# An attention and mixture-of-experts block on one core: query sets by single batches, keys by pairs of batches, the gate's power on GpSimd from tile 2 on, and the last tile's matmuls with the logits' half first

## The reference

```python
x = x + layernorm(attention(layernorm(x)))   # 32 query heads, 8 key heads, head size 16, rotary, causal
x = x + layernorm(ffn(layernorm(x)))
# ffn: x @ W_base.T + b; logits = x @ W_gate.T (8 experts), softmax, top 2, renormalised;
# h = x @ A (8 experts x rank 16), times the route weight of its expert, @ B, added
```

## Time and profile before

| | us |
|---|---|
| median of 3 runs (lowest, highest) | 234.39 (233.6, 234.4) |
| the profiled execution, its own time | 235.09 |
| its span, first to last instruction | 233.4 |
| PE busy | 201.3 (86%) |
| DVE busy | 173.3 (74%) |
| ACT busy | 125.6 (54%) |
| POOL busy | 113.2 (49%) |

### The profile page before, as it was taken

One profiled execution on the slowest core, in us unless ns is written; L12 is line 12 of the kernel. 1 busy time (PEld: TensorE's weight loads), 2 busy tenths in 40 slices (PEclk: granted clock), 3 DMA queues, 4 the chain that ended last, 5 costly groups with the idle time before them and its releaser, 6 DMA issues.

```text
span 233.4 us, 3763 instructions
## 1 busy us (share of the span) xinstructions
PE 201.3 (86%) x1292; PEld 123.5 (53%) x1304; DVE 173.3 (74%) x364; ACT 125.6 (54%) x222; POOL 113.2 (49%) x96
## 2 busy tenths in 40 slices
PE   0499999999787879999999989899889989998860
PEld 0394843444454544444444524144778868997830
DVE  1773525767998897868696884686798898888785
ACT  3231440341214877888766785773577488773321
POOL 8200231562439695798743446462746262433352
PEclk9999999999999999999999999999999999999985
DMA  5998048976996302696673203344330001110113
GB/s 162 383 367 328 0 138 164 233 200 168 202 220 144 66 1 76 165 181 125 143 143 65 48 11 51 101 90 95 51 93 0 3 0 45 46 48 0 45 45 135
DMA packets 22465, 26.73 MB, mean 115 GB/s; under 512 B 3760, under 2 KB 17328, under 8 KB 21680
## 3 DMA queue, kind: packets, MB, share of 16 engines
q1 hardware_dynamic: 22304, 26.38, 44.8%
q10 hardware_dynamic: 144, 0.13, 0.2%
HBM read 17.19 MB, written 6.95 MB: 103 GB/s over the span
## 4 chain that ended last, share of the span: by engine, by line
PE 48%; DVE 22%; ACT 10%; issue 9%; DMA 5%; POOL 3%; SPq 2%; DVEq 0%; POOLq 0%
PE ps L1146 7%; PE ps L1194 7%; PE ps L1131 6%; PE ps L1105 4%; PE ps L1046 4%; PE ps L1169 4%; DVE stats L772 4%; PE ps L1036 3%; DVE nmax L967 3%; PE ps L1022 3%; DVE nmax L964 2%; ACT L577 2%; ACT region_a L719 2%; DMA x_sb<-x 2%; PE ps L1085 2%
## 5 line engine op out<-in xcount | busy, mean ns | idle before, releaser
L543 POOL TENSOR_SCALAR_AFFINE_SELECT region_a<-region_a 128x1024 f32<-128x1024 f32 x32 | 36.9, 1154 | 26.9 <-ACT region_a L719 26.7
L967 DVE TENSOR_REDUCE nmax<-ps 128x4 f32<-128x1024 f32 x32 | 39.1, 1223 | 10.3 <-PE ps L1105 10.0
L719 ACT ACTIVATE region_a<-ps 128x1024 f32<-128x1024 f32 x32 | 32.7, 1022 | 0.2 <-PE ps L1131 0.2
L1036 PE MATMUL ps<-region_a,region_c 128*128 128x512 f32 x64 | 29.0, 598 | 0.0
L1131 PE MATMUL ps<-region_b,kst 98*128 98x512 bf16 x96 | 26.8, 381 | 1.6 <-ACT region_a L719 1.1
L716 ACT ACTIVATE region_a<-ps 128x512 f32<-128x512 f32 x32 | 19.2, 599 | 16.4 <-PE ps L1131 15.9
L964 DVE TENSOR_REDUCE nmax<-ps 128x4 f32<-128x512 f32 x32 | 21.8, 682 | 4.8 <-PE ps L1089 4.4
L1146 PE MATMUL ps<-region_a,v_aug 128*32 128x512 f32 x192 | 25.3, 603 | 0.0
L583 ACT ACTIVATE std<-mv,eps_sb 128x1 f32<-128x1 f32 x32 | 9.3, 293 | 22.4 <-DVE mv L773 22.3
L1105 PE MATMUL ps<-kst,region_b 96*128 96x128 bf16 x256 | 19.6, 219 | 1.4 <-DVE nmax L967 0.8
L462 POOL TENSOR_TENSOR region_a<-region_a 128x512 f32<-128x512 f32 x4 | 6.5, 1627 | 28.9 <-DVE region_a L820 28.9
(11 more groups left out here) (107 smaller groups left out, 415.3 us busy)
## 6 DMA issues: line engine op xcount, KB each, us to landing
q_scr<-region_c SPq DMA_DIRECT2D x24, 128.0 KB, 2.6
region_b<-q_scr SPq DMA_DIRECT2D x8, 384.0 KB, 5.2
x_sb<-x SPq DMA_DIRECT2D x8, 256.0 KB, 5.7
region_b<-q_scr SPq DMA_DIRECT2D x8, 256.0 KB, 5.6
attn_t<-o_sb SPq DMA_DIRECT2D x32, 64.0 KB, 2.4
rden_bc<-r_scr SPq DMA_DIRECT2D x8, 256.0 KB, 3.4
out<-region_b SPq DMA_DIRECT2D x7, 256.0 KB, 2.0
kst<-k_scr SPq DMA_DIRECT2D x8, 192.0 KB, 3.5
```

The costliest lines, as they stand in the source:

```text
L543: pool.affine_select(out=blocks, in_=blocks, compare_op=ALU.is_ge, fill=0.0, base=0, pattern=[[0, 2], [0, REP], [1, P]], channel_multiplie ...
L719: nc.scalar.activation(probs[:, u % PRING, 1:3, :], ps[:, 4:6, :], ACT.Exp, scale=float(HEAD_DIM) ** -0.5).then_inc(exp_done, 1)
L967: nc.vector.tensor_reduce(nmax[:, gi % 2, 1, heads], ps[:, 1:3, :].rearrange("p a (r k) -> p r a k", r=REP), AX.XY, ALU.max, negate=True). ...
L1036: last = nc.tensor.matmul(ps[:, SET_BANKS[i][ri], :], wq_sb[:, c, col:col + P], xn_t[:, c, half * HALF:(half + 1) * HALF], start=(c == 0), ...
```

## The change

Sets are now (kind, index): `("q", b)` is one batch with both groups, `("k", p)` a pair of batches with 256 columns. Order: q0, k0, q1, k1 in front, q2 and q3 in steps 0 to 7 of the loop, a quarter in each. The front's rotation is on VectorE alone; both late sets go over GpSimd. Keys are written without repetition and repeated when loaded, in a ring of three batches. `POWER_TILE` goes from 5 to 2. In the last tile's step TensorE does the second half of the columns first, and `gating_choice` of the last tile moves one step ahead, with its `gate_power`. `attn_low_part` of the last batch moves from step 4 to 5 on GpSimd. The probability slots start at 3 (`slot_of`), and some small tiles share memory.

```diff
+KRING = 3
-LOADS = {7: 4, 15: 5, 18: 6, 22: 7}
+LOADS_Q = {9: 4, 15: 5, 18: 6, 22: 7}
+LOADS_K = {8: 2, 18: 3}
-POWER_TILE = 5
-ROPE_3 = {0: 1, 1: 2}
-MATMULS_4 = (1, 1, 1, 1, 1)
-ROTATE_4, SPLIT_HIGH_4, SPLIT_MIDDLE_4, WRITE_4 = 5, 10, 12, 14
+POWER_TILE = 2
+LATE_PROJECT = 4
+K_ROPE = {0: 0, 1: 1, 2: 2, 3: 3}
+K_HIGH, K_MIDDLE = 2, 3
+LATE_COPY = {2: (2, 0), 4: (2, 1), 6: (3, 0), 8: (3, 1)}
+LATE_ROTATE = {2: 0, 8: 1}
+LATE_HIGH = {6: 4, 10: 5}
+LATE_MIDDLE = {7: 4, 12: 5}
+LATE_WRITE = {7: 2, 14: 3}
...
-        SETS = [(0, 0), "K", (0, 1), (1, 0), (1, 1)]
-        SET_BANKS = [(2, 3), (4, 5), (6, 7), (2, 3), (4, 5)]
+        SETS = [("q", 0), ("k", 0), ("q", 1), ("k", 1), ("q", 2), ("q", 3)]
+        SET_BANKS = [(2, 3), (4, 5), (2, 3), (4, 5), (6, 7), (6, 7)]
...
             sp.dma_start(ident_sb[:, :], ident).then_inc(ident_loaded, 16)
+            sp.dma_start(x_sb[:, 1, :], x[P:2 * P, :]).then_inc(x_loaded[1], 16)
+            sp.dma_start(wq_sb[:, :, :], wq.rearrange("(c p) n -> p c n", p=P)).then_inc(wq_loaded, 16)
+            for t in range(2, TILES):
+                sp.dma_start(x_sb[:, t, :], x[t * P:(t + 1) * P, :]).then_inc(x_loaded[t], 16)
+                if t == 3:
+                    sp.dma_start(tab_sb[:, :, :], tables).then_inc(tab_loaded, 16)
+                    sp.dma_start(wk_sb[:, :, :], wk.rearrange("(c p) n -> p c n", p=P)).then_inc(wk_loaded, 16)
             sp.dma_start(wv_sb[:, :, :], wv.rearrange("(c p) n -> p c n", p=P)).then_inc(wv_loaded, 16)
...
+            def load_k(b):
+                sp.wait_ge(k_written[b], WRITES)
+                if b >= KRING:
+                    sp.wait_ge(t_psum, 2 * KV_HEADS * (b - KRING + 1))
+                for part, (first, count) in enumerate(RUNS):
+                    rows = k_scr[b, part].rearrange("i f h n -> (i f) (h n)")
+                    sp.dma_start(kst[first * HEAD_DIM:(first + count) * HEAD_DIM, b % KRING, :, :],
+                                 rows.unsqueeze(0).broadcast_to([count, HEAD_DIM, KV_HEADS * SEQ]))\
+                        .then_inc(k_loaded[b % KRING], 16)
...
             write_q(0)
+            write_k(0, (0, 1))
             load_q(0)
+            write_k(0, (2,))
+            load_k(0)
+            load_q(1)
+            write_k(1, range(PARTS))
+            write_q(1)
+            load_k(1)
             load_q(2)
             load_q(3)
+            write_k(2, range(PARTS))
+            write_k(3, range(PARTS))
...
 # GpSimd, tile phase
-                if POWER_TILE <= s - 3 < TILES:
+                if POWER_TILE <= s - 3 < TILES - 1:
                     gate_power(s - 3)
+                if s == TILES + 1:
+                    gate_power(TILES - 1)
+                if s == 5:
+                    attn_low_part(BATCH - 1)
...
 # VectorE, front
+            input_tiles(0, 6)
+            dve.wait_ge(tab_loaded, 16)
+            for i in range(2):
+                rope_multiply(i, 0)
+                rope_multiply(i, 1)
+                for piece in (rope_add, rope_left, rope_low):
+                    piece(i, 0)
+                    piece(i, 1)
+            input_tiles(6, TILES)
...
 # VectorE, tile step
                     ln_stats(3, t4, y_sb[:, t4 % 2, :])
+                    if t4 == TILES - 3:
+                        gating_choice(TILES - 1)
...
 # TensorE, front
+            turn_x(0)
+            turn_x(1)
+            project_q(0)
+            turn_x(2)
+            turn_x(3)
+            project_k(0)
+            for t in range(4):
+                project_v(t)
+            project_q(1)
+            for t in range(4, TILES):
+                turn_x(t)
+                if t > 4:
+                    project_v(t - 1)
+            project_v(TILES - 1)
+            project_k(1)
...
 # TensorE, loop
-                if n < len(MATMULS_4):
-                    project(4, 2 * KC - sum(MATMULS_4[n:]), MATMULS_4[n])
+                if n < 2 * LATE_PROJECT:
+                    project_q(2 + n // LATE_PROJECT, (n % LATE_PROJECT,))
...
 # TensorE, tile step
+                if t2 == TILES - 1:
+                    for term in range(3):
+                        base_down_router(t2, term, (1,))
+                    turn_hw(t3)
+                    base_down_router(t2, 0, (0,))
+                    up_projection(t3)
+                    base_down_router(t2, 1, (0,))
+                    turn_hw(t2)
+                    base_down_router(t2, 2, (0,))
+                    up_projection(t2)
+                    return
```

More of the change, by code:

```diff
@@ L50 @@
 RING = 5
+KRING = 3
 PRING = 8
+FIRST_SLOT = 3
 ST_LAG = 9
@@ L184, in build @@
         mask_loaded = sem("mask_loaded")
-        wq_loaded = [sem(f"wq_loaded{g}") for g in range(2)]
+        wq_loaded = sem("wq_loaded")
         tab_loaded = sem("tab_loaded")
@@ new lines, in rope_low @@
+            def rope_low(i, ri):
+                a, cols = i % 2, slice(0, SEQ if SETS[i][0] == "k" else HALF)
+                dve.wait_ge(left, 2 * i + ri + 1)
+                dve.wait_ge(part_m, 2 * i + ri + 1)
+                nc.vector.tensor_tensor(parts[:, a, ri, 2, cols], resid[:, a, ri, cols], parts[:, a, ri, 1, cols],
+                                        ALU.subtract).then_inc(part_l, 1)
+            input_tiles(0, 6)
[6 more added lines that the diff above has]
+                    piece(i, 1)
@@ L1029, in project, with project_q @@
+            def project_q(b, pieces=range(4)):
+                i = SETS.index(("q", b))
+                pe.wait_ge(wq_loaded, 16)
+                pe.wait_ge(xnt_ready, 2 * b + 2)
+                for piece in pieces:
+                    ri, g = divmod(piece, 2)
                     if i == 2:
+                        pe.wait_ge(rope_mul, 2 * ri + 2)
+                    if i == DIRECT:
                         pe.wait_ge(v_ready, 2)
-                    pe.wait_ge(xnt_ready, 4 * half + 4)
-                    for m in range(first, first + count):
-                        ri, c = divmod(m, KC)
-                        col = (2 * g + ri) * P
-                        last = nc.tensor.matmul(ps[:, SET_BANKS[i][ri], :], wq_sb[:, c, col:col + P],
-                                                xn_t[:, c, half * HALF:(half + 1) * HALF],
-                                                start=(c == 0), stop=(c == KC - 1))
@@ L1039, in project @@
-                if first + count == 2 * KC:
-                    last.then_inc(proj_psum, 1)
+                    if i > DIRECT:
+                        pe.wait_ge(late_copied, ri + 1)
+                    col = (2 * g + ri) * P
+                    for c in range(KC):
+                        last = nc.tensor.matmul(ps[:, SET_BANKS[i][ri], g * SEQ:(g + 1) * SEQ], wq_sb[:, c, col:col + P],
+                                                xn_t[:, c, b * SEQ:(b + 1) * SEQ], start=(c == 0), stop=(c == KC - 1))
@@ L1141, in attend @@
                 pe.wait_ge(probs_masked, 4 * gi + 4)
+                if gi == 0 and piece == 0:
+                    pe.wait_ge(late_copied, 4)
                 if gi >= 1 and kt == 0:
@@ L1191, in base_down_router @@
                 act_part, w = ((xn1_h, wcat_h), (xn1_h, wcat_l), (xn1_l, wcat_h))[term]
-                for hf in range(2):
+                for hf in halves:
                     for c in range(KC):
@@ L1251, in _ @@
                     project_out(EARLY_OUT[n])
-            for s in range(2, TILES + 3):
+            for s in range(2, TILES + 2):
                 tile_step(s)
```

467 lines of the change are left out of this document (222 added, 245 removed).

## The result

The changed kernel takes **250.94 us** (median of 4 runs, 249.35 to 251.71), the kernel before 234.39: a ratio of 1.071, 95% interval 1.065 to 1.076. The prediction was 233.0, with 236.3 as its upper end. The profiled execution is the fastest of the four (249.35, span 247.6). A ratio always sets a kernel against runs of the kernel before on the same chip.

What follows compares the result with a forecast made beforehand. Keys and TensorE's queue end the front together; the loop is TensorE's after the first attend, the tile phase TensorE's from step 5. +1.1 (loop) - 1.2 (tile phase) - 1.3 (last tile) = -1.4 from 234.39: 233.0, range 229.9 to 236.3.

Steps and rivals of the forecast that it cites:

- the write (2.05 to 2.6) and three loads put the keys in place at 42 to 44.5: Front: keys land 1.5 to 4 us before they are needed, so the first score comes at 46.1 instead of 54.2.
- No term: Loop, SP: maxima of group 1 come at 32 us after the first score, SP is free at 32.1; no cost.
- Query loads of groups 5 to 7 wait for nothing new: Loop: these query loads get no added wait; no cost was counted.
- a query set 7.0: Front, TensorE's queue: the first one-batch query set takes 7.0 us, from 13.5; the queue is free at 46.0.
- steps of 3.0: Loop, steps 0 to 7: 1.25 us plus a quarter set of 1.76 makes each TensorE step 3.0.
- the second rotation and its stall: Loop, GpSimd: second late set's rotation ends 35.15 after the first score; ScalarE stalls about 3 us, first attend 1.1 later.
- the tile phase's 1.2 and 1.3: Tile phase: 1.2 us less without ScalarE's table loads at step 5; last tile: 1.3 less with its logits first.
- so it moves with the step: Tile step 5: the collision of GpSimd's subtract with a small VectorE operation comes 1.1 us earlier, keeping the 1.1 gain.
- The last tile: Second half of the columns first: VectorE's bias of tile 7 starts 1.3 us earlier, bounds 0.6 and 1.9.
- the port takes the tile phase's gain: Rival, chance 0.10: GpSimd collides with VectorE's small operations; 1.1 and half the last tile's gain lost: +0.4, 234.8.
- The keys come late: Rival, chance 0.17: key loads take 8 us, first score at 50 instead of 46.1: +2.5, 236.9.
- The late sets do not stall the exponentials: Rival, chance 0.25: no stall before the first attend, so the loop keeps its 1.5: -4.0, 230.4.

Runs made afterwards that it cites:

- idle turns: Unread identity transposes on TensorE around the first two turns of x; 16, 6 and 4 of them added to the repaired kernel: 237.55 us, ratio 1.016.
- no slow start and plain loads: The repaired kernel with 22, 16 and 6 idle turns before, between and behind the first two turns of x: 236.97 us, ratio 1.012.
- repaired kernel: The changed kernel with its keys repeated by the write and loaded plainly, 96 rows per batch: 239.72 us, ratio 1.019; once more on another chip 238.81, ratio 1.016.
- tile edits alone: The kernel before with only power from tile 2, the last batch's low part at step 5 and the last tile's logits first: 234.0 us for 234.22, ratio 0.998.

## Why the prediction was wrong, by its steps

Two of its own signs of being wrong came: the first score was limited by the keys, and the first attend moved by 11 us from 89.7.

**Failed: "the write (2.05 to 2.6) and three loads put the keys in place at 42 to 44.5".** The load was priced from rows of a DMA of 96 rows; the changed one has another form, and no row of before had it. They landed near 51.5, with the first score at 51.65. The Trainium skill (DMA: Bandwidth & Descriptors, Rules for kernel authors) has the rule that I did not weigh: a leading broadcast dimension of c copies confines a DMA to at most c engines. The runs agree in what they can show, 251.2 us for 239.72 by the form of the load alone; the number of engines is not seen in them. It was a case of "the diff changes an access pattern, not only its size", and it cost 10 to 12 us.

**Failed: "No term" and "Query loads of groups 5 to 7 wait for nothing new".** I asked when SP could issue, not what lay in the DMA queues ahead. The maxima of group 1 were issued in time (84.0) and the later row landed at 94.9: TensorE waited 2.23 us. For a query load behind the keys of batch 3 it waited 1.96.

**Mis-sized: "a query set 7.0" for the first one.** The set began at 12.66 (forecast 13.5) but took 9.98. The reason was to be read in the trace of the kernel before, in the timeline of TensorE:

```profile
8.74 1.09 PE L1007 MATMUL ps<-ident_sb,region_b 128*128 128x128 f32 x4 [8.74 <-DVE region_b L786]
...
14.95 0.60 PE L1007 MATMUL ps<-ident_sb,region_b 128*128 128x128 f32 x4
```

The same four transposes cost 1.09 at first and 0.60 six microseconds later; the trace's first record of full clock is at 14.6. Before, transposes and values ahead of the set paid for this; a set that starts earlier pays itself, 1.8 to 3.1 us (sets of 8.84 to 10.20 in the profiles without turns). With the loads repaired it moves the first score to 47.3 to 48.7.

**Right: steps of 3.0, the second rotation and its stall.** Steps took 2.89; the rotation ended 36.0 us after the first score (forecast 35.15), ScalarE's casts stood ahead of the exponential, and TensorE waited 2.52 + 0.53 (forecast 3). **Missing** was what followed such a pause: half clock for 3.4 to 10.2 us. With no slow start and plain loads the first attend came 46.2 us after the first score, where I had 43.6: 2.6 us, with 10.2 us of half clock. In the two executions of the repaired kernel, with 3.4 and 6.8, it was 1.1.

**Failed: the tile phase's 1.2 and 1.3.** Shown by the tile edits alone: 0.2 us in the runs, 0.8 in the profile. The step that failed is "so it moves with the step": the collision did not merely move, it now met the residual add too, VectorE's operations came hardly earlier, and TensorE, no longer held up by ScalarE, waited for them (0.72 at the turn of hw, 1.12 for a bias later). The last tile gave the lower bound of its range, 0.6, for the reason given there.

Of the rivals, "the port takes the tile phase's gain" is what happened (it left 0.75 us of the 2.5, where the profile shows 0.8 and the runs 0.2). The Trainium skill (GPSIMD Engine Reference, Specifications), which was cited for it, has the interface shared between the two engines, and this trace agrees: 1.14 and 1.12 us for 0.28 and 0.15. "The keys come late" had the place right but not the size: it allowed 8 us for a landing, the first score at 50 and 236.9 in all, because it took its bound from the same rows of the other form. "The late sets do not stall the exponentials" fell. The prediction missed by 17.9 us (250.9 for 233.0). What the runs show for it: 11.5 for the load's form, 1.8 to 2.9 for the slow start, 2.6 for the loop's pause and half clock beyond the forecast, 1.7 to 2.3 for the tile phase, together 17.6 to 19.3. The parts come from different kernels and need not add exactly; the 2.6 is of one execution. Counted in the changed kernel's own profile, its span of 247.6 misses the predicted 232.0 by 15.6: 2.3 because TensorE's queue was free at 48.28 and not at 46.0, 3.3 for the keys, 5.5 between the first score and the first attend (49.1 us for 43.6), 2.5 in the rest of the loop and 2.0 in the tile phase with the last tile.

**Open:** why runs of one and the same repaired kernel lie up to 7 us apart (233.99 to 240.96 in the widest) while 17 runs of the kernel before kept within 2.3 on each of four chips (15 within 2.8 on the fifth). The runs of lower time mostly have the higher mean clock (0.985 to 0.997 for 0.968 to 0.990), which fits half clock behind a pause in some runs and not in others, and the two profiled executions of the repaired kernel differ so (3.4 us of half clock in the loop and 3.4 at the tile phase's start in one, 6.8 in the loop in the other). But no profile of a run below 236.7 us was taken.

## What to carry to other kernels

When a diff rewrites a DMA, compare the outermost dimension of its access pattern with that of the row that you price it by: here bytes and count said nothing on the change of form, and what was queued behind it paid too. When a step moves earlier, look at what TensorE did in the microseconds ahead of it, both at the start and behind every pause. And a wait that disappears on one engine is worth only the slack of the next one: here VectorE, busy 41.5 of 47.1 us, took it back.

## What the runs showed of the hardware

- One load of 384 KB in 96 rows landed in 3.6 us, six of 64 KB in 2.2 each, one of 256 KB with 16 copies outermost in 3.3; in three pieces with 3, 2 and 1 copies outermost the keys took about 10, and a 128 KB query load behind them 12.5 instead of 6.4.
- TensorE's first matmuls ran at about half rate whatever the granted clock in the row says: in the front of the changed kernel and the repaired ones without turns the column reads 1.00 while the set takes 8.8 to 10.2 us. Where idle turns had run before a pause of 2.91 us, the column shows 0.50 behind it, and a stretch with 7 matmuls in 2 us, for 6 in the changed kernel at the clock of 1.00 that its row gives:

```profile
14.00:16.00 2.00, 2.00 (x7) 1.48 (x6) 1.38 (x5) 0.97 (x3) 0.00 (x0) 0.50 1.12 343
```

- Pauses of 1.85, 2.52 and 3.36 us were each followed by a granted clock of 0.50 (the lower of the two levels, 1.2 GHz); one of 1.28 us in the same kernel as the first was not. The length of a pause does not tell alone: one of 1.96 us in the changed kernel (to 128.36) and one of 1.46 in the repaired one (to 90.05) were not followed by it, while two of 1.35 and 0.67 us close together in the repaired kernel (to 168.37 and 169.67) were.
- VectorE's cast of 32 elements took 0.17 us with GpSimd idle. Beside GpSimd it ended some 0.04 us behind the end of an operation of GpSimd: 0.47 beside a mask (changed kernel, cast to 108.25, mask to 108.22), 0.75 beside a multiply, 1.47 across the end of one mask and the whole of the next. So did the operations of the tile phase: 2.17 to 190.81 beside a subtract to 190.77.
